# Attention front with the delta rule, then a mixture of experts, on one core: normalized input laid out with features on partitions, and TensorE's queue regrouped by array form

## The chip, the cores and the metric

One core of a Trainium2 chip. The metric is the time of one launch in microseconds on that core, all numbers in float32. The time before is the median of three runs.

## What is computed

T is 2048 tokens of D = 512 features, H is 8 heads of 64.

```python
x = x + attn(layernorm(x));  x = x + ffn(layernorm(x))
# attn: q, k, v = silu(conv4(x @ W)); q, k = l2norm(q), l2norm(k); beta = sigmoid(x @ Wb)
def step(S, inp):
    u = b_[..., None] * (v_ - jnp.einsum('bhk,bhkv->bhv', k_, S))
    S = S + jnp.einsum('bhk,bhv->bhkv', k_, u)
    o = jnp.einsum('bhk,bhkv->bhv', q_, S)
# o = o * rsqrt(mean(o*o) + eps) * norm_w;  return o @ Wo
# ffn: 16 experts of width 352, group-limited top 4 of 16, plus a shared expert of width 704
```

The layer norm in front of the attention is (x - mean) / sqrt(var + 1e-5) over the 512 features of a token, with no weights.

## The kernel before

The program has two parts, `attention` and `experts`. The change lies in `attention`, and in the layout of one input.

The 2048 tokens are 16 tiles of 128, or 8 pairs of 256. Every engine walks the same table: u from -8 to 18, and six slots s in each u. Tile u of the recurrence runs in step u (16 steps, from 0 to 15); the steps below 0 are the opening. Work for later tiles is spread over the same slots: in an even u the first six projection chunks of pair (u+6)/2, in an odd u the last six of pair (u+5)/2. A chunk is `project` (L1001): four matmuls of 128*128 weights on 256 tokens, 8 records in the trace since a float32 matmul of this form makes two. What an engine does in a slot, and in which order, stands in its loop.

How a pair's normalized input is made before: SP loads two tiles (`load_x`, L411, slot 0 of an even u), VectorE makes mean and variance (`ln1_stats`, L1430), GpSimd makes r = (var+eps)^-0.5 and -mean*r (`rstd1`, L616, slot 0 of the next, odd u), ScalarE scales the tiles (`make_xn`, L731), TensorE turns them by four 128x128 transposes a tile (`xT`, L975, slots 3 and 4), and ScalarE copies each into `xnT` (`xnT_copy`, L736). In the next even u, slot 0, the first chunk of that pair waits for `xnT`. `betas` (L988) is a product of `xnT` with 8 columns.

TensorE's array takes three other forms in the recurrence. `merge_w` and `merge_x` (L1103, L1115) are 16 products of 32*32 each, `hop_r`, `hop_u_and_scores`, `hop_u`, `hop_o` and `gram` (L1125 to L1207, L1075) are of 64*64, `betas` and `gate` of 128*64. In a step u: slot 5 of u-1 merge_w(u); slot 0 hop_r, a chunk, merge_x; slot 1 a chunk, hop_u with the scores of the next tile, gate; slot 2 hop_o and a chunk; slots 3 to 5 the same for the second half, with the output projection in slot 4. Between them: merge_w, then `w_copy` (L812, ScalarE), then merge_x, then `x_copy` (ScalarE) and `scale_inverse` (GpSimd), then hop_u; hop_u, then `u_copy` (ScalarE), then hop_o.

Every fourth tile needs the inverses of four tiles' gram blocks. VectorE makes them in pieces (`inverse`, mostly in u = 2 mod 4 and 3 mod 4); for tiles 0 to 3 this is in u = -3 and -2. They go through DRAM: `store_inverse` and `store_others` (L428, L433) and then `load_inverse` (L437) for four tiles, six DMAs each. SP issues them in slots 4 and 5 of u = 3 mod 4. For the first four tiles it does so in slot 5 of u=-2 and slot 0 of u=-1:

```python
if opening(u, s) == INVERT + 8:
    store_inverse(0)
    sp.wait_ge(s_vf, 16)
    load_inverse(0)
if opening(u, s) == INVERT + 9:
    store_others(0)
    sp.wait_ge(s_vo, 32)
    for t in range(1, 4):
        load_inverse(t)
```

`opening` counts slots from u=-6, and INVERT is 21. SP's queue is one queue in order; a wait in it holds everything behind it.

## Time and profile before

| | |
|---|---|
| median of 3 runs | 1263.47 us (1261.1 to 1267.51) |
| the profiled execution | 1262.86 us |
| its span in the profile | 1261.1 us |
| TensorE busy | 1223.0 us |
| VectorE busy | 839.0 us |
| ScalarE busy | 365.3 us |
| GpSimd busy | 349.6 us |
| the recurrence (steps 0 to 15) | from about 104 to 525 us |

In the views PE is TensorE's matmuls, PEld its weight loads, DVE VectorE, ACT ScalarE, POOL GpSimd, SP the queue that issues DMAs. A row of the timeline is a start, a length, an engine, a line of the kernel, an operation with what it writes and reads, the form of the array for a matmul, the shape, and how many records it joins. In square brackets stands how long the engine was idle before it and who ended that. The length holds the time to the end of the last record, so the next row can begin before it is over.

### The profile page before, as it was taken

To read this page: it belongs to the slowest core of one execution; us is meant where nothing else is said; L and a number is where in the kernel's file an instruction comes from. 1 tells how busy PE (TensorE), PEld (TensorE's weight loads), DVE (VectorE), ACT (ScalarE), POOL (GpSimd) and SP (SyncE) were. 2 spreads that over 40 slices of the span, in tenths; PEclk is the share of its full clock that TensorE was granted. 3 is DMA by queue.
4 is the path that set the end of the run, shared out by engine and by line. 5 is a ranking of instruction groups with operands and counts; after the bars stand their busy time and mean duration, and the time that the engine had idled before them with its cause. 6 is when DMAs were issued, how large, how long until landed. Compare 5 with 4: busy or idle time off the path is not lost.

```text
span 1261.1 us, 26634 instructions
## 1 busy us (share of the span) xinstructions
PE 1223.0 (97%) x8779; PEld 750.5 (60%) x8779; DVE 839.0 (67%) x2340; ACT 365.3 (29%) x804; POOL 349.6 (28%) x417
## 2 busy tenths in 40 slices
PE   8999989999998999999999999999999999999995
PEld 7887767877776656544444455555555555555553
DVE  5897688769869573344420377777877777777773
ACT  4755645655553323220000011111111111111111
POOL 3411324322332122212564112122222222221222
PEclk9999999999997999999999999999999999999998
DMA  5444953843563396255546777888888887879762
GB/s 169 88 60 98 142 122 78 161 114 86 114 143 128 89 240 139 93 194 192 193 169 245 246 172 179 207 185 221 185 208 200 230 189 175 209 176 235 181 141 26
DMA packets 214307, 202.43 MB, mean 161 GB/s; under 512 B 72608, under 2 KB 154528, under 8 KB 214176
## 3 DMA queue, kind: packets, MB, share of 16 engines
q1 hardware_dynamic: 130080, 112.25, 35.5%
q10 hardware_dynamic: 67456, 54.24, 16.7%
q0 software_dynamic: 16640, 34.24, 13.1%
q8 instruction: 76, 1.25, 0.4%
q14 instruction: 55, 0.45, 0.1%
HBM read 123.76 MB, written 81.08 MB: 162 GB/s over the span
## 4 chain that ended last, share of the span: by engine, by line
PE 55%; DMA 0%; DVE 0%; issue 0%; POOLq 0%; ACT 0%; DVEq 0%
PE pD L2491 13%; PE pG L2478 12%; PE pU L2478 12%; PE pD L2459 4%; PE pG L2440 4%; PE pU L2440 4%; PE pD L2488 2%; PE pG L2474 2%; PE pU L2474 2%; PE pU L2434 1%; PE pD L2454 1%; DMA out<-front_region,ix 0%; DVE ups L2366 0%; POOLq L2161 0%; ACT front_region L2311 0%
## 5 line engine op out<-in xcount | busy, mean ns | idle before, releaser
L2366 DVE STREAM_TRANSPOSE ups<-a 32x96 f32<-32x96 f32 (+1 forms) x1136 | 296.6, 261 | 35.3
L2239 POOL DMA_INDIRECT out<-front_region,ix x64 | 99.3, 1552 | 355.5 <-DMA out<-front_region,ix 169.7
L2491 PE MATMUL pD<-w,ups 128*128 (+1 forms) x384 | 176.5, 595 | 0.7 <-DVE ups L2366 0.7
L2478 PE MATMUL pG<-w,xsT 128*128 x512 | 162.7, 460 | 0.0
L2478 PE MATMUL pU<-w,xsT 128*128 x512 | 161.9, 459 | 0.0
L1010 PE MATMUL pProj<-front_region 128*128 128x256 f32 x624 | 153.8, 389 | 2.2 <-ACT front_region L742 1.6
L2478 PEld LDWEIGHTS pG<-w,xsT 128*128 128x128 f32 x512 | 96.2, 189 | 74.1 <-issue 32.9
L2478 PEld LDWEIGHTS pU<-w,xsT 128*128 128x128 f32 x512 | 97.3, 190 | 54.2
L1010 PEld LDWEIGHTS pProj<-front_region 128*128 128x128 f32 x624 | 112.5, 190 | 20.0 <-ACT front_region L742 2.0
L2491 PEld LDWEIGHTS pD<-w,ups 128*128 128x128 f32 (+1 forms) x384 | 72.0, 190 | 78.9 <-issue 67.9
L2301 ACT ACTIVATE g<-pG 128x352 f32<-128x352 f32 x72 | 33.4, 463 | 285.8 <-issue 120.8
L1452 DVE SCALAR_TENSOR_TENSOR front_region<-front_region,cw 128x256 f32<-128x256 f32 x204 | 97.6, 520 | 8.9 <-ACT front_region L781 6.5
L2311 ACT ACTIVATE front_region<-pD,wq 128x512 f32<-128x512 f32 x72 | 49.5, 687 | 183.8 <-PE pD L2491 129.4
L2400 DVE TENSOR_TENSOR a<-g,pU 128x352 f32<-128x352 f32 x72 | 37.4, 520 | 93.0 <-ACT g L2301 70.3
L2225 POOL DMA_INDIRECT slot_rows<-xall,pos x64 | 61.7, 964 | 57.8 <-DMA slot_rows<-xall,pos 49.5
L665 POOL TENSOR_TENSOR TT<-TT,ng 128x512 f32<-128x512 f32 x16 | 17.5, 1091 | 209.2 <-ACT TT L823 133.9
L1224 PE MATMUL pT<-wo,oT 128*128 128x512 f32 x128 | 59.1, 604 | 0.4 <-ACT oT L850 0.4
L2355 DVE STREAM_TRANSPOSE xsT<-front_region 128x512 f32<-128x512 f32 x72 | 50.6, 703 | 5.3 <-DMA front_region<-slot_rows 5.0
L2459 PE MATMUL pD<-front_region 128*128 128x512 f32 x120 | 53.1, 597 | 0.0
L780 ACT ACTIVATE front_region<-pProj 128x256 f32<-128x256 f32 x76 | 29.3, 386 | 79.1 <-PE pProj L1010 76.8
L1514 DVE TENSOR_TENSOR Rs<-pC,vh 64x512 f32<-64x512 f32 x32 | 22.0, 687 | 45.4 <-PE pC L1135 45.0
L2440 PE MATMUL pG<-front_region 128*128 128x512 f32 x112 | 50.4, 593 | 0.6 <-PEq L401 0.6
(327 smaller groups left out, 1804.2 us busy)
## 6 DMA issues: line engine op xcount, KB each, us to landing
w<-in_expert_T SPq DMA_DIRECT2D x80, 384.0 KB
front_region<-in_expert_T ACTq DMA_DIRECT2D x64, 352.0 KB
slot_rows<-zeros SPq DMA_DIRECT2D x72, 266.0 KB, 7.4
front_region<-slot_rows ACTq DMA_DIRECT2D x288, 64.0 KB
front_region<-in_expert_T ACTq DMA_DIRECT2D x32, 256.0 KB
front_region<-in_L_attn_hidden_states SPq DMA_DIRECT2D x16, 256.0 KB, 3.8
x2r<-in_L_attn_hidden_states SPq DMA_DIRECT2D x16, 256.0 KB, 4.4
partial_sums<-x2r SPq DMA_DIRECT2D x16, 256.0 KB, 3.3
```

The source lines that it names most:

```text
L1010: mm = pe.matmul(proj_bank(g), w3[:, w, k, cols(i % DC, P)], xnT[p % 2][:, k, :], start=(k == 0), stop=(k == DC - 1))
L1224: mm = pe.matmul(pT1[:, 0, :], oT[:, k, :], wo[:, k, :], start=(k == 0), stop=(k == DC - 1))
L1452: ins = dve.scalar_tensor_tensor(out=acc[(g + h) % len(acc)], in0=raw[:, at, j:j + PW], scalar=cw[:, at, j:j + 1], in1=acc[(g + h) % len(a ...
L2225: pool.indirect_dma_start(out=xs_d[:, :], out_offset=bass.IndirectOffsetOnAxis(ap=pos[:, i, j:j + 1], axis=0), in_=xall[:, i, :], in_offse ...
L2239: pool.indirect_dma_start(out=flat, out_offset=bass.IndirectOffsetOnAxis(ap=to[:, 0:1], axis=0), in_=y[(q - 1) % RING][:, :], in_offset=No ...
L2355: dve.transpose(xsT[par][:, :, :].rearrange("p k (a i) -> p a k i", a=BLOCKS), xs[q % RING][:, :].rearrange("p (a k j) -> p a k j", a=BLOC ...
L2366: dve.transpose(aT[par][B * to:B * to + B, 0:n, rows], a[rows, 0:len(IC) * P].rearrange("p (c n) -> p c n", c=len(IC))[:, 0:n, B * to:B * ...
L2440: mm = pe.matmul(p[:, :], wsh["up"][:, k, at:at + P], xg[gr % 2][:, k, :], start=(k == 0), stop=(k == DC - 1))
L2459: mm = pe.matmul(sdown(j)[:, :], sa[:, c, P * i:P * i + P], wsh["down"][:, c, :], start=False, stop=(c == UNITS - 1))
L2474: mm = pe.matmul(out[half, 0:I], rows[:, k, half], wm[:, h, 2 * I * k + at:2 * I * k + at + I], start=(k == 0), stop=(k == DC - 1))
L2478: mm = pe.matmul(out[:, 0:I], rows[:, k, :], w[:, bass.ds(weights[0], 1), 2 * I * k + at:2 * I * k + at + I], start=(k == 0), stop=(k == D ...
L2491: return pe.matmul(out[:, :], gated_[0:m, c, :], w[0:m, bass.ds(weights[0], 1), at:at + D], start=(c == 0), stop=(c == 2))
```

## The change

The host lays the input out a second time, `x_T`, with features on partitions, for each pair 128 x (4 x 256). For pairs 2 to 7 (`TURNED = 2`) SP loads this straight into `xnT` (`load_columns`, slot 1 of the even u = 2p-8; slot 4 of u=-4 for pair 2). The statistics are still made from rows. r and -mean*r now lie in one tile `rows1` of 128x4; SP stores it to DRAM (`store_rows1`, slot 1 of the odd u = 2p-7), waits for that, and loads it back spread over all partitions into `xin[0]` (`spread_rows1`, slot 2). GpSimd then multiplies `xnT` by r and adds -mean*r (`scale_columns`, slot 3), two operations on 128x1024 in place. For these pairs `make_xn`, the turns and `xnT_copy` are gone.

TensorE's queue is regrouped. merge_x now stands directly behind hop_r and ahead of the chunk of slot 0; the first chunk of a step goes to a bank of `pG`, the scores' own, so that two chunks stand together in front of hop_u. betas moves behind hop_u (slot 1), the second k turn of an odd step above 0 from slot 1 to slot 2 (and `k_rows`, `k_sums` and `coefs` with it), merge_w behind the turns of slot 5. ScalarE makes x_copy ahead of the chunk's copy and w_copy ahead of the SiLUs.

```diff
     st1, mv1 = sb("st1", [P, 2, 6]), sb("mv1", [P, 2, 2])
-    r1, nm1 = sb("r1", [P, 2]), sb("nm1", [P, 2])
+    rows1 = sb("rows1", [P, 4])
+    r1, nm1 = rows1[:, 0:2], rows1[:, 2:4]
...
+    rows1_d = dram("ln1_rows", (1, P * 4))
...
+    TURNED = 2
...
+    def late_turn(u):
+
+        return 2 if u > 0 else 1
...
+    def ahead_of_scores(g):
+
+        return g >= EARLY and (g % SLOTS == 0 or g == 3 * DC * PAIRS - 2)
+
+    def first_chunk(u):
+
+        pk, pq = (u + 6) // 2, (u + 5) // 2
+        if u + 4 == NT - 2:
+            return 3 * DC * PAIRS - 2
+        if u % 2 == 0 and pair_ok(pk):
+            return 3 * DC * pk
+        if u % 2 and pair_ok(pq):
+            return 3 * DC * pq + SLOTS
+        return None
+
     def proj_bank(g):
 
+        if ahead_of_scores(g):
+            return pG[:, 0, 0:PW]
         return pC[:, 0, 0:PW] if g < EARLY and g % 2 else pProj[:, 0, 0:PW]
 
...
             def load_x(t):
-                least(sp, s_xTp, t - 1)
+                least(sp, s_xTp, min(t, 2 * TURNED + 1) - 1)
+                if t // 2 > TURNED:
+                    sp.wait_ge(s_xnT, 2 * (t // 2))
                 sp.dma_start(xin[t % 2][:, :], xv[t]).then_inc(s_xl[t % 2], 16)
+
+            def load_columns(p):
+
+                sp.wait_ge(s_proj, place(p - 2, 3 * DC - 1) + 1)
+                sp.wait_ge(s_bp, p - 1)
+                sp.wait_ge(s_xnT, 2 * p)
+                sp.dma_start(xnT[p % 2][:, :, :], xTp_d[p].rearrange("p (c n) -> p c n", c=DC)).then_inc(s_xcl, 16)
+
+            def store_rows1(p):
+                sp.wait_ge(s_xcl, 48 * (p - TURNED) + 16)
+                sp.wait_ge(s_r1, p + 1)
+                sp.dma_start(rows1_d.rearrange("o (p n) -> (o p) n", n=4), rows1[:, :]).then_inc(s_xcl, 16)
+
+            def spread_rows1(p):
+
+                sp.wait_ge(s_xcl, 48 * (p - TURNED) + 32)
+                sp.dma_start(xin[0][:, :], rows1_d.to_broadcast([P, P * 4])).then_inc(s_xcl, 16)
 
             def store_gram(t):
...
+                    if even and s == (4 if u == -4 else 1) and TURNED <= (u + 8) // 2 < PAIRS:
+                        load_columns((u + 8) // 2)
+                    if not even and TURNED <= (u + 7) // 2 < PAIRS:
+                        if s == 1:
+                            store_rows1((u + 7) // 2)
+                        if s == 2:
+                            spread_rows1((u + 7) // 2)
...
-                        sp.wait_ge(s_xTp, NT)
+                        sp.wait_ge(s_st1, NT)
...
             def rstd1(p):
                 pool.wait_ge(s_st1, 2 * p + 2)
-                least(pool, s_xn, 2 * p)
+                least(pool, s_xn, 2 * min(p, TURNED))
+                if p > TURNED:
+                    pool.wait_ge(s_xcl, 48 * (p - TURNED))
                 link(pool.tensor_scalar(r1[:, :], mv1[:, :, 1], LN_EPS, None, ALU.add))
                 link(pool.tensor_tensor(r1[:, :], r1[:, :], nhalf[:, 0:2], ALU.pow))
                 link(pool.tensor_tensor(nm1[:, :], mv1[:, :, 0], r1[:, :], ALU.mult))
                 pool.tensor_scalar(nm1[:, :], nm1[:, :], -1.0, None, ALU.mult).then_inc(s_r1, 1)
+
+            def by_token(j):
+
+                return grid(xin[0], 2 * j, (0, DC), (1, 2), (4, P))
+
+            def scale_columns(p):
+                pool.wait_ge(s_xcl, 48 * (p - TURNED + 1))
+                both = xnT[p % 2][:, :, :].rearrange("p c (i n) -> p c i n", n=P)
+                link(pool.tensor_tensor(both, both, by_token(0), ALU.mult))
+                pool.tensor_tensor(both, both, by_token(1), ALU.add).then_inc(s_xnT, 2)
...
+                    if s == 3 and not even and TURNED <= (u + 7) // 2 < PAIRS:
+                        scale_columns((u + 7) // 2)
...
             def xnT_copy(t):
                 p = t // 2
                 act.wait_ge(s_xTp, t + 1)
-                if p >= 2:
-                    act.wait_ge(s_proj, place(p - 2, 3 * DC - 1) + 1)
-                least(act, s_bp, p - 1)
...
+                    if tile_ok(u) and s == 0 and u < FUSED:
+                        x_copy(u)
...
-                    if tile_ok(u) and s == 0 and u < FUSED:
-                        x_copy(u)
-                    if even and s == (0 if pk else 1) and pair_ok(pk) and pk != 1:
+                    if s == 5 and tile_ok(u + 1):
+                        w_copy(u + 1)
+                    if even and s == 1 and pair_ok(pk) and pk != 1:
...
-                    if not even and pair_ok((u + 5) // 2) and s in (0, 1) and u != -3:
-                        k_rows(u + 5 + s)
-                    if not even and pair_ok(new) and new != 1:
+                    if not even and pair_ok((u + 5) // 2) and s in (0, late_turn(u)) and u != -3:
+                        k_rows(u + 5 + (s > 0))
...
-                elif t % 2 == 0:
-                    least(pe, s_ksq, 2 * p)
-                    if t == 4:
-                        pe.wait_ge(s_qsq, 2)
-                else:
...
-                if p == 1:
-                    pe.wait_ge(s_ksq, 2)
+                least(pe, s_ksq, 2 * p)
+                if p == 2:
+                    pe.wait_ge(s_qsq, 2)
...
-            def project(g):
+            def project(g, u=None):
                 p, i = chunk(g)
                 w = (1, 2, 0)[i // DC]
                 if i == 0:
                     pe.wait_ge(s_xnT, 2 * p + 2)
                 if p == 0 and i % DC == 0:
                     pe.wait_ge(s_w3[w], 16)
-                least(pe, s_raw, 2 * g if g >= EARLY else 2 * g - 2)
+                if ahead_of_scores(g):
+                    scores_wait(u + 1)
+                    pe.wait_ge(s_PT, u + 1)
+                else:
+                    least(pe, s_raw, 2 * g - 2 if g < EARLY or ahead_of_scores(g - 1) else 2 * g)
...
+                if first_chunk(t) is not None:
+                    pe.wait_ge(s_raw, 2 * first_chunk(t) + 2)
...
+                    if s == 0 and tile_ok(u):
+                        merge_x(u)
                     if even and pair_ok(pk):
-                        project(3 * DC * pk + s)
+                        project(3 * DC * pk + s, u)
...
-                        if tile_ok(u):
-                            merge_x(u)
                         if u + 3 == NT - 2:
                             qT(NT - 1)
-                        if even and pair_ok(pk) and pk > 1:
-                            betas(pk)
                         if not even and pair_ok(pq) and pq != 1:
                             kT(2 * pq)
                     if s == 1:
-                        if not even and pair_ok(pq) and pq != 1:
-                            kT(2 * pq + 1)
                         if tile_ok(u - 3):
                             gate(u - 3)
+                        if even and pair_ok(pk) and pk > 1:
+                            betas(pk)
+                    if s == late_turn(u) and not even and pair_ok(pq) and pq != 1:
+                        kT(2 * pq + 1)
...
-                        if not even and pair_ok(new) and new != 1:
+                        if not even and new == 0:
                             xT(2 * new)
...
                     if s == 5:
-                        if tile_ok(u + 1):
-                            merge_w(u + 1)
                         if even and pair_ok(old) and 0 < old < PAIRS - 1:
                             (qT if old in LATE else vT_turn)(2 * old + 1)
                         if even and old == PAIRS - 1:
                             qT(2 * old)
+                        if tile_ok(u + 1):
+                            merge_w(u + 1)
...
-                        if s in (1, 2) and pq != 1 and not late_gram(u):
-                            k_sums(2 * pq + s - 1)
-                            if s == 2:
+                        if s in (1, late_turn(u) + 1) and pq != 1 and not late_gram(u):
+                            k_sums(2 * pq + (s > 1))
+                            if s > 1:
                                 coefs(pq)
...
+            laid['x_T'] = laid[n].reshape(PAIRS, PW, DC, P).transpose(0, 3, 2, 1).reshape(PAIRS, P, DC * PW)
```

SP's queue around u=-1, before. TT and NP are the buffers that the inverse is loaded into, slot_rows is cleared with zeros, gram_blocks takes a tile's gram.

```order
L449 DMA NP2<-inverse_rows 32x8x32
L443 DMA TT2<-inverse_turned 32x8x32
L449 DMA NP2<-inverse_rows 32x8x32
L443 DMA TT3<-inverse_turned 32x8x32 x3
L449 DMA NP3<-inverse_rows 32x8x32
L443 DMA TT3<-inverse_turned 32x8x32
L449 DMA NP3<-inverse_rows 32x8x32
L474 DMA slot_rows<-zeros 512x1x133
L419 DMA gram_blocks<-NP4 32x8x32 x4
```

The same place now. L451 is the store of pair 3's rows, L456 their spread.

```order
L492 DMA NP2<-inverse_rows 32x8x32
L486 DMA TT2<-inverse_turned 32x8x32
L492 DMA NP2<-inverse_rows 32x8x32
L486 DMA TT3<-inverse_turned 32x8x32 x3
L492 DMA NP3<-inverse_rows 32x8x32
L486 DMA TT3<-inverse_turned 32x8x32
L492 DMA NP3<-inverse_rows 32x8x32
L451 DMA ln1_rows<-rows1 128x4
L456 DMA front_region<-ln1_rows 128x512
L517 DMA slot_rows<-zeros 512x1x133
L462 DMA gram_blocks<-NP4 32x8x32 x4
```

Two DMAs are new there, behind the last load of the inverse.

TensorE around the start of tile 0, before: a chunk, merge_w, hop_r, a chunk, merge_x, betas, a chunk.

```order
L1010 MATMUL pC<-front_region 128x256 x4
L1111 MATMUL pT1<-TT0,NP0 32x32 x16
L1135 MATMUL pC<-S,kq0 64x64 x8
L1010 MATMUL pProj<-front_region 128x256 x4
L1121 MATMUL pT1<-Wt,NP0 32x32 x16
L997 MATMUL pT0<-wb,front_region 64x8 x16
L1010 MATMUL pProj<-front_region 128x256 x4
```

And now:

```order
L1072 MATMUL pC<-front_region 128x256 x4
L1173 MATMUL pT1<-TT0,NP0 32x32 x16
L1197 MATMUL pC<-S,kq0 64x64 x8
L1183 MATMUL pT1<-Wt,NP0 32x32 x16
L1072 MATMUL pG<-front_region 128x256 x4
L1072 MATMUL pProj<-front_region 128x256 x4
```

merge_x has moved ahead of the chunk, the two chunks are neighbours, and betas comes later. The chunk into pG is the first of pair 3.

## Rows read from the trace of the kernel before

**Rows 1.** The page: busy us (share of the span) xinstructions of each engine.

```profile
span 1261.1 us, 26634 instructions
PE 1223.0 (97%) x8779; PEld 750.5 (60%) x8779; DVE 839.0 (67%) x2340; ACT 365.3 (29%) x804; POOL 349.6 (28%) x417
```

**Rows 2.** Timeline of TensorE in tile 4: start us, us, engine, line, operation.

```profile
212.40 1.99 PE L1010 MATMUL pProj<-front_region 128*128 128x256 f32 x8
214.32 0.69 PE L1121 MATMUL pT<-Wt,NP 32*32 32x32 f32 x32
...
221.33 1.99 PE L1010 MATMUL pProj<-front_region 128*128 128x256 f32 x8
223.16 0.60 PE L972 MATMUL pT<-ident,x2n 128*128 128x128 f32 x4
223.59 0.60 PE L972 MATMUL pT<-ident,front_region 128*128 128x128 f32 x4
224.12 0.69 PE L1084 MATMUL pG<-kq 64*64 64x64 f32 x32
```

**Rows 3.** The same view: waits of TensorE in tiles 0, 2 and 4.

```profile
112.56 0.59 PE L1187 MATMUL pC<-S,kq 64*64 64x64 f32 x13 [0.77 <-ACT Us L830]
...
182.70 0.69 PE L1111 MATMUL pT<-TT,NP 32*32 32x32 f32 x32 [2.38 <-DVE x2r L1535]
...
220.28 0.59 PE L1187 MATMUL pC<-S,kq 64*64 64x64 f32 x13 [0.20 <-ACT Us L830]
```

**Rows 4.** Busy time by stretch: the opening, tile 3, tile 5.

```profile
core 0: us, PE busy (x) PEld busy (x) DVE busy (x) ACT busy (x) POOL busy (x), PEclk, DMA share, GB/s
50.00:75.00 25.00, 25.00 (x181) 21.49 (x180) 22.26 (x55) 16.29 (x49) 3.17 (x9) 1.00 0.93 136
75.00:100.00 25.00, 24.00 (x181) 20.47 (x181) 24.34 (x38) 15.01 (x44) 6.80 (x10) 1.00 0.13 24
...
183.91:211.32 27.41, 26.74 (x385) 21.05 (x385) 24.01 (x38) 15.16 (x33) 11.60 (x17) 1.00 0.38 96
...
239.33:266.51 27.18, 27.18 (x418) 21.54 (x417) 17.69 (x36) 17.01 (x40) 11.21 (x19) 1.00 0.61 120
```

**Rows 5.** Timeline of SP's queue around the first inverse.

```profile
94.05 0.34 SPq L430 DMA_DIRECT2D inverse_turned<-route_keep  x1
...
99.34 0.43 SPq L435 DMA_DIRECT2D inverse_rows<-route_keep  x1
104.86 1.30 SPq L443 DMA_DIRECT2D TT<-inverse_turned  x3
...
116.84 0.52 SPq L474 DMA_DIRECT2D slot_rows<-zeros  x1
```

**Rows 6.** Timelines of TensorE, ScalarE and GpSimd in the opening.

```profile
104.67 1.99 PE L1010 MATMUL pProj<-front_region 128*128 128x256 f32 x8
106.60 0.69 PE L1121 MATMUL pT<-Wt,NP 32*32 32x32 f32 x32
...
104.51 0.75 ACT L817 ACTIVATE Wt<-pT 32x256 f32<-32x256 f32 x2
...
57.53 0.47 POOL L622 TENSOR_SCALAR nm<-nm 128x2 f32<-128x2 f32 x1
93.59 0.46 POOL L622 TENSOR_SCALAR nm<-nm 128x2 f32<-128x2 f32 x1
```

**Rows 7.** DMA issues: count, KB of each, median us from issue to landing.

```profile
front_region<-in_L_attn_hidden_states SPq DMA_DIRECT2D x16, 256.0 KB, 3.8
x2r<-in_L_attn_hidden_states SPq DMA_DIRECT2D x16, 256.0 KB, 4.4
...
x_normed<-x2n SPq DMA_DIRECT2D x16, 256.0 KB, 3.1
...
gram_blocks<-NP SPq DMA_DIRECT2D x64, 32.0 KB, 2.1
```

**Rows 8.** Groups of instructions: busy us, mean ns of one, idle before.

```profile
L665 POOL TENSOR_TENSOR TT<-TT,ng 128x512 f32<-128x512 f32 x16 | 17.5, 1091 | 209.2 <-ACT TT L823 133.9 <-PE pT L1111 75.3
```

**Rows 9.** Timelines of VectorE, GpSimd and TensorE at the start of tile 4.

```profile
208.59 0.68 DVE L1535 TENSOR_TENSOR x2r<-x2r,pT 128x512 f32<-128x512 f32 x1
...
213.11 2.69 DVE L1452 SCALAR_TENSOR_TENSOR acc_more<-front_region,cw,acc_more 128x256 f32<-128x256 f32 x6
215.72 3.50 DVE L1452 SCALAR_TENSOR_TENSOR front_region<-front_region,cw 128x256 f32<-128x256 f32 x6
...
215.91 1.20 POOL L665 TENSOR_TENSOR TT<-TT,ng 128x512 f32<-128x512 f32 x1 [8.02 <-ACT TT L823]
...
210.70 0.69 PE L1111 MATMUL pT<-TT,NP 32*32 32x32 f32 x32
```

**Rows 10.** Busy time by stretch, PEclk is the granted clock as a share of 2.4 GHz.

```profile
398.00:402.00 4.00, 4.00 (x69) 3.43 (x68) 3.90 (x8) 1.82 (x4) 2.56 (x5) 0.50 0.18 63
...
406.00:410.00 4.00, 4.00 (x12) 1.47 (x12) 3.93 (x6) 0.38 (x1) 2.94 (x4) 0.50 0.17 66
```

More of the change, by code:

```diff
@@ L204, in least, with attention @@
         eng.wait_ge(sem, n)
-def attention(nc, es, x_d, wq_d, wk_d, wv_d, wb_d, cq_d, ck_d, cv_d, nw_d, wo_d, gw_d, shu_d, shd_d, region, wsh,
+def attention(nc, es, x_d, xTp_d, wq_d, wk_d, wv_d, wb_d, cq_d, ck_d, cv_d, nw_d, wo_d, gw_d, shu_d, shd_d, region, wsh,
               route, sh, lg, acc_d, x2n_d, xT_d, xs_d, out):
@@ L961, in _ @@
                         oT_copy(u - 1)
-                    if s == 5 and tile_ok(u + 1):
-                        w_copy(u + 1)
                     for i, (lo, n, at_u, at_s) in enumerate(ROUTES):
@@ L1322, in _ @@
             for i in range(WARM):
-                mm = pe.matmul(pS[:, 0, cols(i % 2, P)], zeros[:, 0:P], zeros[:, 0:P], start=(i == 0), stop=False,
+                pe.matmul(pS[:, 0, cols(i % 2, P)], zeros[:, 0:P], zeros[:, 0:P], start=(i == 0), stop=False,
                                skip_group_check=True)
-            mm.then_inc(s_zS, 1)
             for u in range(FIRST, LAST):
@@ L1396, in _ @@
                             vT_turn(2 * old + 1)
-                        if not even and pair_ok(new) and new != 1:
+                        if not even and new == 0:
                             xT(2 * new)
@@ L1403, in _ @@
                             (qT if old in LATE else vT_turn)(2 * old)
-                        if not even and pair_ok(new) and new != 1:
+                        if not even and new == 0:
                             xT(2 * new + 1)
@@ L2544, in _, with program @@
             run_slots(pe, body)
-def program(nc, x, wq, wk, wv, wb, cq, ck, cv, nw, wo, gw, wex, shu, shd, out):
+def program(nc, x, x_T, wq, wk, wv, wb, cq, ck, cv, nw, wo, gw, wex, shu, shd, out):
     with ExitStack() as es:
@@ L2585, in program @@
         with ExitStack() as inner:
-            attention(nc, inner, x, wq, wk, wv, wb, cq, ck, cv, nw, wo, gw, shu, shd, region, wsh, route, sh, lg, acc_d,
+            attention(nc, inner, x, x_T, wq, wk, wv, wb, cq, ck, cv, nw, wo, gw, shu, shd, region, wsh, route, sh, lg, acc_d,
                       x2n_d, xT_d, xs_d, out)
@@ L2601 @@
     nc = bacc.Bacc("TRN2", target_bir_lowering=False, num_devices=1)
-    laid = {n: np.asarray(inputs[n]) for n in _INS}
+    laid = {}
+    for n in _INS:
+        laid[n] = np.asarray(inputs[n])
+        if n == _INS[0]:
+            laid['x_T'] = laid[n].reshape(PAIRS, PW, DC, P).transpose(0, 3, 2, 1).reshape(PAIRS, P, DC * PW)
     laid['gate_T'] = np.asarray(inputs['L0_ffn_gate_w']).T
```

13 lines of the change are left out of this document (7 added, 6 removed).

## The prediction

> **What bounds the kernel now.** I read the engine table first [rows 1]: TensorE is busy 97% of the span and no other engine above 67%, so time is what TensorE's queue takes plus where it waits. All of the change lies in the attention front, roughly the first 400 us. There the time-ordered list of TensorE shows pieces of one kind start to start [rows 2]: a projection chunk of 8 records takes 1.83 us when the next piece is also of 128 rows and columns (221.33 to 223.16) and 1.92 when it is of 32 (212.40 to 214.32); a turn of one tile takes 0.43 before another turn and 0.53 before 64*64 work. So leaving a form costs about 0.1 us; with the other side of the run (merging a gram with the 64*64 hop behind it) I take 0.15 per change of form.
>
> TensorE's waits are few. Behind hop_u it waits for ScalarE's copy: 0.77 us at 112.56 with nothing between, 0.20 at 220.28 with a gate between [rows 3]. Before merge_w of tile 3 it waits 2.38 us for VectorE's x2 [rows 3]. That wait shows the second resource: in the stretch of tile 3 VectorE is busy 24.01 of 27.41 us, against 17.69 of 27.18 two tiles on [rows 4].
>
> The third resource is SP's queue, in order. When the first inverse is ready, SP issues two stores at 94.05, waits for the second pair until 104.86, and comes to the next DMA, behind 24 loads in all, only at 116.84 [rows 5]. TensorE starts the first chunk of pair 3 at 104.67 [rows 6]. Nothing in that chunk depends on this burst before.
>
> **The change, part by part.**
>
> *Turns taken away.* Pairs 2 to 7 lose 12 turns (48 transposes), 12 x 0.43 = 5.2 us of TensorE. Four of them (pairs 2 and 3) lie ahead of the place below, where time is set by something else; 8 x 0.43 = 3.4 us count. ScalarE loses 24 activations; it is 29% busy and waits for TensorE, so that is nothing.
>
> *Regrouping.* By the order lists the changes of form on TensorE in the whole program go from 276 to 253. Of the 23, some 19 lie where TensorE is the bound: 19 x 0.15 = 2.9 us. betas now stand behind hop_u, where the 0.77 us waits were at tiles 0 and 2, and at tiles 4, 6, 8 the 0.20; the k turn has gone from there in odd tiles, which opens such waits (0.77 at tile 1, 0.20 at 3, 5, 7, 9). Counted over tiles 0 to 10 that is 2.5 us of waits before and 1.7 after: 0.8 us gained. merge_x directly behind hop_r needs w_copy done: merge_w ends, ScalarE copies for 0.75 us [rows 6], hop_r covers 0.6 (tile 0) to 1.1 us, and the copy now stands ahead of the SiLUs: nothing, at most 0.3 us a tile. The first chunk in a bank of pG waits for mask and grams that were done long before: nothing.
>
> *The new chain for a pair.* VectorE's statistics, four small GpSimd operations, SP stores the 128x4 rows, waits for them, spreads them to 128 partitions, waits; GpSimd multiplies and adds 128x1024; then the pair's first chunk. Prices: store 2.1 us (nearest: a 32 KB store to DRAM), spread 3.8 (256 KB from DRAM; bounds 3.1 and 4.4) [rows 7]. GpSimd's 128x512 takes 1.09 us [rows 8], so two of 128x1024 make 4 x 1.09 = 4.4 us; from below the same, from above 6.6, since one operand steps over 16 bytes and no row has that. The Trainium skill, GPSIMD Engine Reference, section "Performance pitfalls for Q7 kernels", puts about 50% more on reads that step over more than 8 bytes; by it the pass would take 6.6 us and the sum below be 2.2 us longer. For pairs 4 to 7 the chain starts about 9 us into an odd tile of 27 us and needs some 12, so it ends before the next tile: no wait.
>
> *Pair 3 is the exception, and decides the sum.* Its row store is in slot 1 of u=-1. On SP's queue that is behind the whole inverse burst, which is issued in slot 5 of u=-2 and slot 0 of u=-1. The rows themselves are ready at 94.05 (93.59 + 0.46) [rows 6]; they will leave only when SP has passed the burst. Sum:
> - burst starts at 94.05 before. VectorE is nearly full from 50 to 100 us (46.6 of 50) [rows 4], and GpSimd's pass for pair 2 (about 64 to 68.5) now runs beside it. Six conv operations take 3.50 us with a 1.20 us GpSimd product beside them and 2.69 without [rows 9]: 0.8 us lost per 1.09 us of product, so up to 3.2 for 4.4 us; not all of VectorE's work there is of that kind, I take 2.5 (bounds 0 and 3.8): 96.5.
> - burst and waits 116.84 - 94.05 = 22.8: 119.3. Store 2.1: 121.4. Spread 3.8: 125.2. GpSimd 4.4: 129.6.
> - TensorE can have done merge_x (0.62) meanwhile, so against 104.67 it is 24.9 - 0.6 = 24.3 us late.
>
> This leaves TensorE idle for about 25 us, and hop_u, all grams and everything else is queued behind. Pair 2 also waits, about 2 us near 66, since its chain starts at 58 (57.53 + 0.47) [rows 6]; that is absorbed by the wait for pair 3 and not counted.
>
> *The clock.* After idle near 394 the granted clock was 0.50 (1.2 instead of 2.4 GHz) from 398 to 410 [rows 10]; 12 us at half speed cost 6. Behind the long wait I expect part of it: 3 us (bounds 0 and 6). The fall at 398 itself may come or not in the new order: down to -6, which is in the range.
>
> *Given back.* In tiles 2, 3, 6 and 7 VectorE is nearly full [rows 4], and GpSimd's pass for pairs 5 and 7 falls into tiles 3 and 7. There x2 is ready 1.4 us before merge_w wants it (208.59 + 0.68 against 210.70) [rows 9]; TensorE comes about 1.2 us earlier, VectorE 2 to 3 us later. So what was gained in these tiles is waited away: 2 us each, 4 in all (bounds 0 and 8). Here the Trainium skill, SBUF — State Buffer, section "SBUF: two separate sides", is harsher than my row: a VectorE operation with two SBUF inputs and a GpSimd operation exclude each other for their whole length. By it VectorE would lose all of the 4.4 us per pass and this term be about 7.
>
> Sum: 24.3 + 3 - 3.4 - 2.9 - 0.8 + 4 = +24.2. The profiled execution took 1262.86 us (span 1261.1 and 1.8 around it) [rows 1], 0.6 under the median of the three runs: 1287 us.
>
> Low end: no VectorE delay (-2.5), faster DMAs (-1), no clock loss (-3), nothing given back (-3), and the old clock fall gone (-6): about 1272. High end: GpSimd at 6.6 (+2.2), delay 3.8 (+1.3), clock 6 (+3), given back 8 (+4): about 1298.
>
> **Rivals.**
> - *The row chain of pair 3 is not held by SP (faster).* The place is the row store of pair 3. It decides if the pass ends before about 105: then 12 turns 5.2, regrouping 3.4, waits 0.8, less 4 given back: 1257 us, and 1253 if nothing is given back. For it: rows ready at 94.05 plus 2.1 + 3.8 + 4.4 = 104.4, just in time if SP were free. Against it: one queue, in order, with 24 loads ahead of the store in the order list. Chance 0.10.
> - *A shorter hold.* The burst's 12 us of issue behind 104.86 might be quicker when TensorE is idle; with half of it and of the wait before it gone, 11 us less: 1276. It shares the mechanism; chance 0.06 for a time below 1275.
> - *GpSimd becomes the bound.* With 6.6 us a pass and full exclusion of VectorE, all six passes hurt: pair 3 later by 2.2 + 1.3, four saturated tiles by 3 us more each, the odd tiles' hop_u by a us each: 1300 or more. Both rules named above point this way. Chance 0.08.
> - *Forecast as worked out*: 0.76.
>
> Half a per cent, 6 us, is about what a measurement of this kernel tells from no change. Faster by more: 0.08; within: 0.04; slower by more: 0.88.
>
> **What would show it.** Right: in the trace after, a wait of TensorE of 20 to 27 us before the first chunk of pair 3 at about 105, released by GpSimd; SP's row store directly behind the inverse loads at 117 to 120; from there to the experts less time than before by 0 to 7 us. Wrong: no TensorE wait over 5 us in the front; or the GpSimd product far from 2.2 us each; or VectorE's conv operations of equal length beside it. If the wait is there but the total is below 1270, the turns and forms are worth more than I read.

## The result

The changed kernel takes 1291.19 us (median of 4 runs, 1287.65 to 1292.9) against 1265.0 us of the kernel before (4 runs): a ratio of 1.0213, 95% interval 1.0188 to 1.0239. It is slower by 26 us. The forecast was 1287, in a range of 1272 to 1298. The profiled execution took 1292.59 us, its span is 1290.8.

The page's engine table, to hold against [rows 1]:

```profile
span 1290.8 us, 26571 instructions
PE 1224.1 (95%) x8731; PEld 753.1 (58%) x8731; DVE 852.2 (66%) x2340; ACT 355.2 (28%) x780; POOL 387.5 (30%) x429
```

TensorE has 48 records less and is as long busy as before; the span is 29.7 us longer, so the loss is idle time. GpSimd has 12 operations more and 38 us more.

The waits of TensorE from 60 to 400 us (waited for, in total, times, longest):

```profile
PE pG L1072 <- POOL front_region L684: 19.4, 1, 19.4
PE pProj L1072 <- POOL front_region L684: 6.6, 1, 6.6
PE pT L1173 <- DVE x2r L1598: 4.3, 2, 2.3
PE pT L1033 <- DVE vh L1552: 2.3, 3, 1.3
```

L684 is GpSimd's addition of -mean*r. The 19.4 us stand before the first chunk of pair 3, the 6.6 before that of pair 2. The two waits for x2r stand before merge_w of tiles 4 and 8.

SP's queue around the first inverse, to hold against [rows 5]:

```profile
101.75 0.34 SPq L473 DMA_DIRECT2D inverse_turned<-route_keep  x1
...
107.05 0.42 SPq L478 DMA_DIRECT2D inverse_rows<-route_keep  x1
112.61 1.31 SPq L486 DMA_DIRECT2D TT<-inverse_turned  x3
...
121.66 0.45 SPq L492 DMA_DIRECT2D NP<-inverse_rows  x1
122.21 0.40 SPq L451 DMA_DIRECT2D ln_rows<-rows  x1
124.42 0.33 SPq L456 DMA_DIRECT2D front_region<-ln_rows  x1
```

Then GpSimd (first three rows, the first of them the last step of the rows) and TensorE, to hold against [rows 6]:

```profile
101.31 0.46 POOL L674 TENSOR_SCALAR rows<-rows 128x2 f32<-128x2 f32 x1
...
128.15 2.85 POOL L683 TENSOR_TENSOR front_region<-front_region 128x1024 f32<-128x1024 f32 x1 [18.81 <-DMA front_region<-ln_rows]
131.14 2.85 POOL L684 TENSOR_TENSOR front_region<-front_region 128x1024 f32<-128x1024 f32 x1
```

```profile
113.92 0.69 PE L1183 MATMUL pT<-Wt,NP 32*32 32x32 f32 x32
134.05 3.61 PE L1072 MATMUL pG<-front_region 128*128 128x256 f32 x8 [19.44 <-POOL front_region L684]
```

The rows of pair 3 are ready at 101.77 and leave at 122.21, directly behind the last load of the burst. Everything behind that is the chain's own length.

VectorE beside GpSimd's pass for pair 2 (68.78 to 75.14):

```profile
67.26 5.17 DVE L1515 SCALAR_TENSOR_TENSOR front_region<-front_region,cw 128x256 f32<-128x256 f32 x6
72.36 2.90 DVE L1617 TENSOR_TENSOR prod_a<-front_region,route_keep 128x100 f32<-128x100 f32 x1
```

Six conv operations take 5.17 us; alone they took 2.69 [rows 9]. The 128x100 product takes 2.90 us; the same line at 128x144, just behind the pass, takes 0.31. Of a pass of 5.9 us VectorE loses about 5.1, all in front of the inverse. The rows of pair 2 were also 2.6 us later (60.60 against 57.53 + 0.47 [rows 6]). That is not tied to the columns: in the experiments below they are ready between 57.4 and 61.6, at 60.3 in the kernel that only regroups. Together that is the 7.7 us by which SP's burst starts later, 101.75 against 94.05.

**Where the 29.7 us of the profiled spans lie.** A mark in each tile is the start of merge_x. At tile 1 the changed kernel is 28.0 us late (158.46 against 130.46); from there to tile 10 it takes 248.98 us against 247.63; behind that the two differ by 0.4. So nearly all of the loss is made before tile 1, and what the turns and the regrouping give is lost again between tiles 1 and 10.

### The profile page after: what moved, and what is told of

It is laid out like the page before. It is cut to its first block, busy times and chain, and to the rows that moved or that the text cites. A ratio compares the mean times of both kernels' runs of the same rounds, so it can differ in the third digit from the quotient of the medians.

```text
span 1290.8 us, 26571 instructions
## 1 busy us (share of the span) xinstructions
PE 1224.1 (95%) x8731; PEld 753.1 (58%) x8731; DVE 852.2 (66%) x2340; ACT 355.2 (28%) x780; POOL 387.5 (30%) x429
## 4 chain that ended last, share of the span: by engine, by line
PE 53%; DMA 0%; DVE 0%; issue 0%; POOLq 0%; ACT 0%; DVEq 0%
PE pD L2554 13%; PE pG L2541 12%; PE pU L2541 12%; PE pD L2522 4%; PE pG L2503 4%; PE pU L2503 4%; PE pD L2551 2%; PE pG L2537 2%; PE pU L2537 1%; PE pU L2497 1%; PE pD L2517 0%; DMA out<-front_region,ix 0%; DVE ups L2429 0%; POOLq L2224 0%; ACT front_region L2374 0%
## 5 line engine op out<-in xcount | busy, mean ns | idle before, releaser
L1072 PE MATMUL pProj<-front_region 128*128 128x256 f32 x536 | 134.2, 394 | 10.1 <-POOL front_region L684 6.6
L1072 PEld LDWEIGHTS pProj<-front_region 128*128 128x128 f32 x536 | 99.4, 194 | 27.1 <-POOL front_region L684 7.0
L2503 PE MATMUL pU<-front_region 128*128 128x512 f32 x112 | 50.3, 592 | 0.0
```

The source lines that it names most:

```text
L1072: mm = pe.matmul(proj_bank(g), w3[:, w, k, cols(i % DC, P)], xnT[p % 2][:, k, :], start=(k == 0), stop=(k == DC - 1))
L2503: mm = pe.matmul(p[:, :], wsh["up"][:, k, at:at + P], xg[gr % 2][:, k, :], start=(k == 0), stop=(k == DC - 1))
```

## The experiments

The first theory: the loss is SP's burst in front of pair 3's rows, plus pair 2's wait; the rest of the change gains a little and gives it back through VectorE. The main rival: columns and GpSimd's passes cost in every pair, and the long wait is only where it shows. Ratios are to the kernel before in the same set of runs. Its median was 1261.5 us in the first set, 1262.3, 1264.3 and 1264.0 in the later ones, so across sets ratios are compared and not times.

**1. The rows of pair 3 ahead of the burst.**

```diff
 (u=-1, slots 1 and 2: store_rows1(3), spread_rows1(3) left out)
+                        store_rows1(3)
                         store_inverse(0)
+                        spread_rows1(3)
                         sp.wait_ge(s_vf, 16)
```

> Only the place of pair 3's two row transfers on SP's queue is changed: the store of the rows goes ahead of the inverse burst, the spread directly behind the burst's first two stores. Theory 1 (the burst on SP's queue holds pair 3, and this hold is the larger part of the loss): rows ready near 101.8, landed 104.2, spread landed about 110, GpSimd's pass of 5.9 done at 116; TensorE, which comes at 113.9, waits about 2 to 4 us instead of 19.4, and the time falls by 14 to 17 us to 1275 to 1277. Theory 2 (the clock and GpSimd's passes beside VectorE cost as much as the wait, and the place of the two transfers matters little, since the pass only moves onto VectorE's full stretch): the wait goes, but the time falls by less than 8 us, to 1283 or more.

Measured: 1270.98 us (1268.87 to 1272.01), ratio 1.0068 (1.005 to 1.0086), that is by the ratios about 18 us less than the changed kernel. SP's queue and GpSimd's last product in that run:

```profile
102.14 0.33 SPq L451 DMA_DIRECT2D ln_rows<-rows  x1
...
103.55 0.34 SPq L456 DMA_DIRECT2D front_region<-ln_rows  x1
```

```profile
112.16 2.86 POOL L686 TENSOR_TENSOR front_region<-front_region 128x1024 f32<-128x1024 f32 x1
```

The pass ends at 115.0 instead of 134.0, and TensorE waits 0.80 us for it. Two transfers in another place of one queue are worth two thirds of the loss. Theory 1 holds. A wait that I had not seen appears behind it: 1.9 us before the first chunk of pair 4.

**2. Pairs 2 and 3 turned again, and no columns at all.** `TURNED = 4`, and then `TURNED = 8`, with the turns' waits as they were before:

```diff
-    TURNED = 2
+    TURNED = 4
...
-                    if not even and new == 0:
+                    if not even and pair_ok(new) and new != 1 and new < TURNED:
```

> Pairs 2 and 3 are turned by TensorE as in the kernel before; columns are loaded for pairs 4 to 7 only; the regrouped queue of TensorE stays. Theory 1 (the two waits in the opening stretch, 19.4 and 6.6 us, make the loss): both are gone, the arrival at the second tile is that of the kernel before within 1 us, and the whole is level with the kernel before or up to 4 us faster: 1261 to 1265. Theory 2 (the columns cost in every pair, through GpSimd's passes beside VectorE): 1270 or more. What is left between this kernel and the one that only regroups is the price of the columns for pairs 4 to 7.

> No columns at all: every pair is turned by TensorE as before; only the order of TensorE's queue (merge_x ahead of the chunk, betas behind hop_u, merge_w last, the k turn two slots on, the first chunk in a bank of pG) and ScalarE's order that goes with it stay. By the sum of the prediction (fewer changes of form 2.9, waits behind hop_u 0.8): 1261, that is 3 to 4 us under the kernel before. Rival: the 0.1 us that a change of form seemed to cost is covered or given back behind VectorE: within 1 us of the kernel before. Second rival: the new order sets waits of its own: slower by 2 us or more.

Measured: pairs 4 to 7 by columns, 1265.45 us, ratio 1.0029 (1.0015 to 1.0043); regrouping alone, 1257.51 us, ratio 0.9965 (0.9951 to 0.9979). The arrival at tile 1 is within 0.3 us of the kernel before with pairs 2 and 3 turned (130.71): all of the 28 us came from these two pairs. But the whole is 0.3% slower than the kernel before, where theory 1 had it level or faster, and 8 us lie between it and the one that only regroups, although it has 8 turns less. The first theory's "the rest gains a little" falls; for pairs 4 to 7 the rival is right.

**3. The passes of pairs 4 to 7 cut.** Each is cut to a quarter of its columns, so the kernel leaves out part of these pairs' layer norm; what stands in front of the passes stays.

```diff
             def scale_columns(p):
...
+                if p > 3:
+                    both = both[:, 0:1]
```

> The changed kernel, with GpSimd's multiply and add of pairs 4 to 7 cut to a quarter of their columns (so these pairs' layer norm is left out in part, with wrong values). Everything in front of them stays. Theory 1 (the passes take VectorE's time and this comes back as waits before merge_w in tiles 3 and 7 and as idle stretches behind which the clock falls): 4 to 8 us less, 1283 to 1287, the two waits of 2.0 and 2.3 us gone. Rival (the passes lie beside the work and cost nothing; the gain of turns and regrouping is lost otherwise): within 1.5 us of the changed kernel.

Measured: 1281.7 us (1277.53 to 1282.64), ratio 1.0151 (1.0128 to 1.0174), 0.6% or 8 us under the changed kernel. The windows view over the same work, merge_x of tile 1 to merge_x of tile 10, in four kernels (stretch, its length, then busy us and count of TensorE, weight loads, VectorE, ScalarE, GpSimd, then granted clock, DMA share, GB/s). Before:

```profile
130.46:378.09 247.63, 239.33 (x3557) 188.89 (x3556) 191.90 (x372) 137.97 (x330) 81.83 (x130) 1.00 0.59 119
```

Regrouping alone:

```profile
129.85:372.48 242.63, 236.77 (x3559) 189.75 (x3557) 193.26 (x372) 141.39 (x332) 83.94 (x126) 1.00 0.56 121
```

The changed kernel with the passes cut:

```profile
156.79:396.66 239.87, 233.15 (x3526) 185.81 (x3525) 193.73 (x368) 131.35 (x316) 90.04 (x134) 1.00 0.54 123
```

The changed kernel:

```profile
158.46:407.44 248.98, 238.18 (x3527) 189.43 (x3525) 198.93 (x368) 131.75 (x316) 107.03 (x134) 0.98 0.55 119
```

Read down the second number: regrouping gives 5.0 us, the eight turns 2.8, and the four passes take 9.1. They take 17 us of GpSimd, and VectorE is busy 5.2 us longer for the same work. In the changed kernel TensorE waits 4.8 us for x2r in this stretch, with the passes cut 0.6.

The 5.0 of regrouping are of two kinds. 2.6 us are TensorE's busy time (239.33 against 236.77), as the price per change of form has it. The other 2.4 are idle time, and I had not forecast them: the kernel before waits 5.0 us for x2r in this stretch, 2.38 and 2.02 of them before merge_w of tiles 3 and 7. With merge_w behind the turn these two waits are gone and 0.6 is left, while the waits for vh grow from 1.3 to 2.9.

Part of the 9.1 is clock. In the changed kernel the two waits for x2r are followed by this (tile 4, then tile 8):

```profile
239.00:241.00 2.00, 2.00 (x61) 1.88 (x60) 0.87 (x3) 1.83 (x5) 0.00 (x0) 0.69 0.82 264
241.00:243.00 2.00, 2.00 (x18) 1.67 (x14) 1.93 (x5) 0.98 (x3) 0.75 (x1) 0.50 0.12 21
243.00:245.00 2.00, 2.00 (x6) 1.55 (x6) 2.00 (x4) 0.00 (x0) 1.75 (x4) 0.50 0.36 55
245.00:247.00 2.00, 2.00 (x7) 1.60 (x6) 1.93 (x6) 1.27 (x3) 0.58 (x2) 0.60 0.46 71
```

```profile
355.00:357.00 2.00, 2.00 (x37) 1.69 (x37) 1.91 (x5) 1.83 (x5) 0.01 (x1) 0.70 0.28 90
357.00:359.00 2.00, 2.00 (x7) 1.56 (x6) 1.96 (x4) 0.00 (x0) 1.83 (x3) 0.50 0.33 51
```

The granted clock is at 0.50 (1.2 GHz) while TensorE is full. Two us times what is missing to 1.00, summed, is 0.6 + 1.0 + 1.0 + 0.8 = 3.4 us in tile 4 and 0.6 + 1.0 = 1.6 in tile 8. With the waits themselves, 1.99 and 2.29 us, that is 9.3 us, about all of the 9.1. So the price of four passes is two waits behind a late VectorE and the slow clock behind them. The kernel before had waits as long in front of the same operation, 2.38 us one tile earlier [rows 3] and 2.02 at 294.92, with no fall behind them; what made the difference here stays open.

**4. Why the passes cost in tiles 3 and 7.** VectorE in tile 3, in the kernel with pairs 2 and 3 turned; GpSimd's pass runs from 201.08 to 207.77:

```profile
202.59 2.44 DVE L1675 TENSOR_TENSOR prod_a<-route_keep,zc 128x1024 f32<-128x1024 f32 x1
205.07 1.22 DVE L1681 TENSOR_REDUCE route_keep<-prod_a 128x64 f32<-128x1024 f32 x1
206.32 1.68 DVE L1740 COPY route_keep<-route_keep 128x256 f32<-128x256 f32 x1
```

The same three with regrouping alone, no pass beside them:

```profile
199.42 1.23 DVE L1675 TENSOR_TENSOR prod_a<-route_keep,zc 128x1024 f32<-128x1024 f32 x1
200.68 1.22 DVE L1681 TENSOR_REDUCE route_keep<-prod_a 128x64 f32<-128x1024 f32 x1
201.94 0.38 DVE L1740 COPY route_keep<-route_keep 128x256 f32<-128x256 f32 x1
```

A product of two tiles in SBUF takes 1.21 us more and the copy 1.30 more; the reduction, with one operand, nothing. If this theory is right, a pass costs only where VectorE is full. I tried that by columns for pairs 4 and 6 alone, whose passes lie in tiles 1 and 5:

```diff
-    TURNED = 2
+    COLUMNS = (4, 6)
...
-                        zero_rows()
+                        if not (u in (0, 4) and s >= 3) and not (u in (1, 5) and s < 2):
+                            zero_rows()
+                            if u in (2, 6):
+                                zero_rows()
```

The second piece moves ten fills; it is the change of experiment 6 and is told there.

> Columns for pairs 4 and 6 alone, the others turned, fills as in the first run of this set. The passes then lie in tiles 1 and 5, where VectorE has idle time, and none in tiles 3 and 7, where it is nearly full. Theory 1 (the price of a pass depends on whether VectorE is full beside it): four turns less at 0.43 against 1257.5, so 1255 to 1257, the fastest so far. Theory 2 (each pass costs about 1.7 us wherever it lies): 1259 or more.

Measured: 1256.74 us (1251.72 to 1262.47, 12 runs), ratio 0.9943 (0.9922 to 0.9963), the lowest of all that compute the whole, under the kernel before and the changed one. Its stretch from tile 1 to tile 10:

```profile
128.41:369.49 241.08, 235.03 (x3542) 187.68 (x3540) 193.26 (x372) 136.62 (x324) 94.83 (x130) 1.00 0.64 129
```

VectorE is busy 193.26 us, what it was without any pass, though GpSimd works 11 us more; the clock is 1.00. This profiled execution took 1253.27 us, 3.5 under the median, so its stretch flatters a little. The closest neighbour is the kernel with columns for 4 to 7 and the same fills moved (experiment 6), in the same set: 1265.36 us. Turning pairs 5 and 7 again gives 8.6 us, and there cutting all four passes instead, with their row chains kept, gives 9.8. So two passes beside a VectorE with idle time cost nothing that these runs show, theory 1, and those in tiles 3 and 7 carry the price.

**5. The rows' two DMAs issued by ScalarE.** First on the changed kernel, then with pairs 2 and 3 turned:

```diff
-                sp.wait_ge(s_r1, p + 1)
-                sp.dma_start(rows1_d...
+                act.wait_ge(s_r1, p + 1)
+                act.dma_start(rows1_d...
```

> The changed kernel with the store and the spread of the rows issued by ScalarE instead of SP, for all six pairs. In the run with the rows ahead of the burst pair 4's store was issued behind four fills of slot_rows on SP's queue and took 11.0 us to the spread (144.46 to 155.46) where other pairs take 2.3, and TensorE waited 1.9 us. Theory 1 (both holds are those of SP's queue, its order and what its DMAs have ahead of them): pair 3 as in that run (pass done near 116), pair 4's wait gone as well, so 2 to 4 us less than that run's 1271: 1267 to 1269. Theory 2 (the fills fill the DMA engines themselves, so another engine's queue waits just as long): pair 4's store takes 8 us or more from here too, 1271 or more. Third possibility: ScalarE's own copies come late because it waits for the rows: new waits of TensorE for ScalarE, 1272 or more.

> Pairs 2 and 3 turned by TensorE, columns for 4 to 7, the rows' store and spread issued by ScalarE. Against the same kernel with SP issuing them (1265.5): its wait of 1.7 us before the first chunk of pair 4 and the slower chunk behind it (3.13 instead of 1.83 us) should go, so 1262 to 1263. If this stays at 1265, that wait was not what pair 4 cost. In no case as fast as the kernel that only regroups (1257.5), if GpSimd's passes beside VectorE cost 4 to 7 us; if it reaches 1259 or less, the passes cost little and the columns pay.

Measured: 1283.6 us (ratio 1.0175, 1.015 to 1.02) and 1269.78 us (ratio 1.0055, 1.0034 to 1.0075). Neither came out as theory 1 has it; the third possibility did. Theory 1 was right for pair 3 alone: its pass is done at 117.2 and TensorE waits 1.2 us for it. ScalarE's queue in tile 1, first run:

```profile
146.81 0.33 ACTq L783 DMA_DIRECT2D ln_rows<-rows  x1
...
157.47 0.33 ACTq L788 DMA_DIRECT2D front_region<-ln_rows  x1
157.84 0.38 ACT L890 ACTIVATE S<-pS 128x256 f32<-128x256 f32 x1 [8.75 <-DMA ln_rows<-rows]
```

SP's queue beside it, and TensorE:

```profile
139.20 10.06 SPq L507 DMA_DIRECT2D slot_rows<-zeros  x6
```

```profile
158.28 1.12 PE L1197 MATMUL pC<-S,kq 64*64 64x64 f32 x16 [5.56 <-ACT S L890]
```

ScalarE waits 8.75 us for its own 2 KB store, its copy of S comes late, and TensorE stands for 5.56 us. The store takes 10.7 us from issue to the spread although nothing is ahead of it on ScalarE's queue: six fills of 266 KB, issued by SP, are on the DMA engines. So theory 2 was right on the fills, and theory 1 wrong for pair 4. By the Trainium skill, DMA: Bandwidth & Descriptors, section "Issuing engines are not separate DMA queues", DMAs run on the same 16 engines whoever issues them; the trace agrees.

**6. The fills moved, and both at once.** `zero_rows` fills the slot rows of the experts, 266 KB each; ten of 72 are issued one tile later, as in the diff of experiment 4.

> Pairs 2 and 3 turned, columns for 4 to 7, SP issues the rows, as in the run of 1265.5; only the fills of slot_rows that SP issued in the two places ahead of the rows of pairs 4 and 6 (ten of them) are issued in the tile behind. Theory 1 (the fills in front of it held pair 4's row store for 11 us, and TensorE's 1.7 us wait and slow chunk come from that): store to spread 2 to 3 us, no wait before the first chunk of pair 4, 3 us less: 1262 to 1263. Theory 2 (the store lands late for other reasons, or the wait only moves): 1265 or more.

> The kernel of 1265.5 with GpSimd's multiply and add of pairs 4 to 7 cut to a quarter of their columns (layer norm left out in part, wrong values). Regrouping alone gave 1257.5; eight turns less are worth 3.4 us; so with passes that cost nothing and no other price this would be 1254. Theory 1 (the passes take VectorE's time in tiles 3 and 7, and the clock falls behind the waits that come of it): 1256 to 1260, the waits before merge_w in tiles 3 and 7 back to under 0.6 us. Rival (the price is the row chain itself, its wait and its DMAs): 1263 or more.

> Fills moved and the passes of pairs 4 to 7 cut, both at once (values wrong as above). Theory 1: nothing is left but eight turns less: 1254 to 1255. If it is 1257 or more, taking the turns away is worth less than 3.4 us, whatever the chain costs.

Measured, against 1.0029 with neither in the earlier set: fills moved 1.0008 (0.9991 to 1.0026), 1265.36 us; passes cut 0.9997 (0.9976 to 1.0018), 1264.07 us; both 0.9927 (0.9901 to 0.9953), 1255.59 us. Fills moved: store to spread is 3.7 us, pair 4's wait is gone, as theory 1 has it; the ratio is 0.2% lower, with intervals that overlap. With both, the eight turns are won and next to nothing is paid for them: 1254 to 1255 was expected on the first set's scale, a ratio of 0.9941 to 0.9948, and 0.9927 came. Alone, cutting the passes gave 4 us where 5 to 9 were expected, and the profiled execution (1267.07 us, 3.0 above the median of its kernel) shows a wait that may be the reason. SP, VectorE and TensorE of that run:

```profile
139.74 2.12 SPq L451 DMA_DIRECT2D ln_rows<-rows  x1
141.90 0.79 SPq L517 DMA_DIRECT2D slot_rows<-zeros  x1
152.63 0.33 SPq L456 DMA_DIRECT2D front_region<-ln_rows  x1
```

```profile
170.71 0.17 DVE L1627 COPY route_keep<-front_region 128x4 f32<-128x4 f32 x1 [7.59 <-DMA front_region<-gram_blocks]
```

```profile
178.71 0.24 PE L1249 MATMUL pC<-Rs,TT 64*64 64x64 f32 x1 [4.07 <-DVE Rs L1591]
```

SP stands 10 us in its own wait for the row store. Grams queued behind it on SP leave late, the lanes of the next inverse come late, VectorE idles 7.59 us for them, and TensorE then waits 4.07 us for VectorE. A wait put into a queue can cost what is behind it, two steps on. It need not: in the kernel of experiment 2 SP stands 9.3 us in the same place, ends 3.4 us earlier, and VectorE, which comes 2 us later, waits only 0.38 us for these lanes. One execution of each does not show how much of the missing gain this is.

**7. Control: regrouping with the fills moved.**

> Control for the run with columns for pairs 4 and 6: no columns at all, the queue regrouped, the ten fills moved. From merge_x of tile 1 to merge_x of tile 10 the kernel before takes 247.63 us, regrouping alone 242.63, columns for 4 and 6 with the fills moved 241.08. Theory 1 (the four turns taken away are the gain, 4 x 0.43 = 1.7): this stretch stays at 242.6 and the whole comes at regrouping's ratio to the kernel before, 0.9965 (about 1259 to 1260 on this chip's scale). Theory 2 (moving the fills made the gain, the turns nothing): 241.1 in the stretch and a ratio near 0.994.

Measured: 1261.04 us, ratio 0.9976 (0.9963 to 0.9989); tile 1 to tile 10:

```profile
129.50:374.08 244.58, 237.19 (x3559) 189.69 (x3557) 192.96 (x372) 141.19 (x332) 83.36 (x126) 1.00 0.62 121
```

Neither theory: moving the fills gains nothing by itself, and this one execution is 2 us longer in the stretch than without it. So the gain of experiment 4 is that of the columns, not of the fills. By the ratios it is 0.9943 against 0.9976, whose intervals only touch at 0.9963. By this stretch it is 3.5 us for four turns, by regrouping alone 1.6; 4 x 0.43 would be 1.7. Against regrouping alone, the intervals of the two ratios (0.9922 to 0.9963 and 0.9951 to 0.9979) overlap, so that columns for 4 and 6 beat it is likely and not shown.

**8. The rows with a step of 4 bytes.** With pairs 2 and 3 turned and ScalarE issuing:

```diff
-                sp.dma_start(rows1_d.rearrange("o (p n) -> (o p) n", n=4), rows1[:, :]) ...
+                act.dma_start(rows1_d.rearrange("o (n p) -> (o p) n", n=4), rows1[:, :], ...
...
-                return grid(xin[0], 2 * j, (0, DC), (1, 2), (4, P))
+                return grid(xin[0], 2 * P * j, (0, DC), (P, 2), (1, P))
```

> As the run beside it, and the four row values of a token are stored so that GpSimd's second operand steps over 4 bytes instead of 16. The store is then of 512 pieces of 4 bytes, which may take a microsecond or two longer. Theory 1 (the 16-byte step makes the product of 128x1024 take 2.87 us instead of 2.2): 2.1 to 2.3 us each, VectorE gets back 1.3 us per pass, and the whole is 1 to 3 us faster than its neighbour. Theory 2 (the product takes 2.87 us for other reasons, such as its three-dimensional operand): still 2.8 to 2.9 us each, and no difference.

Measured: 1298.42 us, ratio 1.0281 (1.0253 to 1.0309), a miss as a kernel, since the store of 512 pieces of 4 bytes now takes 19 us to the spread in tile 1 and 10 in tile 3:

```profile
136.02 0.41 ACTq L784 DMA_DIRECT2D ln_rows<-rows  x1
...
155.09 0.34 ACTq L789 DMA_DIRECT2D front_region<-ln_rows  x1
155.48 0.38 ACT L894 ACTIVATE S<-pS 128x256 f32<-128x256 f32 x1 [17.10 <-DMA ln_rows<-rows]
```

But it answers on the product: 2.35 to 2.59 us, where it is 2.85 to 2.98 with 16 bytes. Theory 1 is right in direction: the step costs some 0.5 us of 2.9, where it had 0.7.

## Why the forecast was right, and where it was not

- **"Pair 3 is the exception, and decides the sum": right, in mechanism and size.** The store of its rows does stand directly behind the burst, and moving it alone gave about 18 us back.
- **The signs that I had named: the place fits, the sizes miss.** The wait stands before the first chunk of pair 3 and GpSimd ends it, but it is 19.4 us, not 20 to 27, since TensorE was already late by pair 2's wait when it came there; SP's row store is at 122.2, not 117 to 120; from tile 1 on the kernel takes 1.7 us more, not 0 to 7 less. GpSimd's product, 2.85 us here, is not near 2.2, which I had called a sign of being wrong; VectorE's conv operations are longer beside it, as forecast.
- **Its terms, from 129.6 forecast to 134.05 measured.** Burst start 96.5 forecast, 101.75 measured: +5.3. Burst and waits 22.8, measured 20.5: -2.3. Store and spread 5.9, measured 128.15 - 122.21 = 5.9. GpSimd's pass 4.4, measured 5.9: +1.5. Together +4.5.
- **The burst's start: mis-sized.** I took 2.5 us of VectorE's delay, at most 3.8, from one row in which it had lost 0.8 us beside 1.09 us of product. VectorE lost 5.1 us of 5.9, and the statistics came 2.6 us later in this execution. I had worked with a share of loss per us of GpSimd; the right term is the whole length of the pass, where VectorE's work is products of two SBUF tiles.
- **Pair 2: "waits ~2 us, absorbed ... not counted": too small, and the rule of absorption only half right.** TensorE waited 6.59 us: the rows came 2.6 us later than I had them, the spread took 5.8 instead of 3.8 (63.02 to 68.78) and the pass 6.4 instead of 4.4. Its own idle time is indeed covered by the wait for pair 3, but what pair 2's pass does to VectorE moves the burst, and with it the end of that wait.
- **GpSimd's pass, 4.4 with 6.6 as upper bound: between.** 5.9 us, of which experiment 8 gives about 1.0 to the step (two products, 0.5 each). The other 0.5 is not explained. The Trainium skill, GPSIMD Engine Reference, "Performance pitfalls for Q7 kernels", has half again as much for steps above 8 bytes; here it is about a fifth (2.87 against 2.36).
- **Regrouping 2.9 and hop waits 0.8: both borne out, and a third part missed.** Alone it gave 0.35% or 4.4 us. TensorE's busy time in tiles 1 to 10 fell by 2.6, near the 2.9. The hop waits fell by 0.8, all of it at tile 0: 1.0 us from 104 to 130 before, 0.2 after; in tiles 1 to 10 they stay (1.5 and 1.6). The 2.4 us of idle time there, from the waits for x2r that went with merge_w's new place, stood nowhere in my sum.
- **Eight turns, 3.4: about right.** 2.8 us with the passes cut.
- **"Given back in tiles 2, 3, 6 and 7 +4 (bounds 0 and 8)": the step that failed most.** The passes took 9.1 us. The waits came where forecast, before merge_w behind tiles 3 and 7, 1.99 and 2.29 us, about the 2 each that I had, and VectorE lost 5.2 us in two passes, 2.6 each, inside my 2 to 3. What I had not is the slow clock behind the waits, 3.4 and 1.6 us.
- **The clock behind the long wait, 3 (0 to 6): 1.7.** The windows there:

```profile
130.00:134.00 4.00, 0.00 (x0) 0.00 (x0) 0.00 (x0) 0.00 (x0) 3.86 (x3) 0.50 0.53 84
134.00:136.00 2.00, 1.95 (x5) 1.59 (x6) 0.00 (x0) 0.00 (x0) 1.28 (x3) 0.50 0.62 138
136.00:138.00 2.00, 2.00 (x8) 1.65 (x7) 0.00 (x0) 0.30 (x2) 0.00 (x0) 0.66 0.95 194
138.00:140.00 2.00, 2.00 (x31) 1.56 (x30) 0.00 (x0) 1.02 (x4) 0.00 (x0) 1.00 0.69 160
```

It is at 0.50 in the idle time and back 3.3 us behind its end: a wait of 19 us cost less clock than one of 2. The old fall near 400 [rows 10] did not go; it stands at 427 to 441 with 0.52.

```profile
427.00:441.00 14.00, 12.79 (x180) 9.48 (x182) 13.73 (x20) 4.35 (x8) 6.81 (x9) 0.52 0.22 70
```

- **The rivals.** "Not held by SP" falls with the order of SP's rows. "A shorter hold" came in part, 2.3 us instead of 11. "GpSimd becomes the bound" (1300 or more) was too strong in its sum, but its mechanism, the exclusion, worked in pair 2 and in tiles 3 and 7. By the Trainium skill, SBUF — State Buffer, "SBUF: two separate sides", VectorE operations with two SBUF inputs, or in a mode that uses both ports, and a GpSimd operation lock each other out for a whole instruction. The products (+1.21 and +2.64 us) agree, and the copy fits; I had spread the rule over all of VectorE's work, and the reductions pay nothing.

The sum by these: 24.2 forecast, chain +4.5, passes +5.1, turns +0.6, regrouping and its waits -1.3 (5.0 for 3.7), clock behind the long wait -1.3, makes 31.8, against 29.7 between the two profiled spans; 2.1 us are not placed. The medians are 26 us apart, nearer to the forecast than the two profiled executions. Errors of both signs cancelled in part, and the number was better than its parts.

## What to carry to other kernels

A DMA that an engine waits for is priced with its place in the issuing queue and with the bulk transfers in flight, not with its size: here 2 KB took 2.2 us in one place, 11 behind fills, and was held 20 us behind a burst. Before handing elementwise work to GpSimd, look at what VectorE does in that very stretch: the same pass was free in tiles 1 and 5 and cost an estimated 4.5 us each in tiles 3 and 7 (half of 9.1), more than half of it clock. And before putting a wait into a shared queue, list what is queued behind it: the harm can show on an engine that neither issues nor waits for that transfer.
